# Row maxima of causal attention: a max pass over 11 and 9 slots in place of 7, turned by VectorE and sent in eight pieces by ScalarE's queue

## The reference

```python
def _L0_attn_ref(x, ids, Wq, Aq, Bq, Wk, Ak, Bk, Wv, Av, Bv, Wo, Ao, Bo):
    Q, K, V = multilora(x, ids, Wq, Aq, Bq), multilora(x, ids, Wk, Ak, Bk), multilora(x, ids, Wv, Av, Bv)
    Q, K, V = split(Q), split(K), split(V)              # (8, 16, 512, 32)
    Q, K = rope(Q), rope(K)
    scores = einsum('bhqd,bhkd->bhqk', Q, K) / sqrt(32)
    scores = where(causal, scores, -inf)
    attn = softmax(scores, axis=-1)
    out = einsum('bhqk,bhkd->bqhd', attn, V).reshape(b, s, 512)
    return multilora(out, ids, Wo, Ao, Bo)

def _L0_ffn_ref(hidden, ...):
    x = rmsnorm(hidden, ln1_w)
    mod = 0.1 * tanh(attention(x, Wq, Wk, Wv, Wo) @ A)  # the same causal attention, 16 heads of 32
    h = rmsnorm(hidden, ln2_w)
    gate = silu(h @ W_in.T + mod * (h @ A) @ B)
    return hidden + (gate * (h @ W_up.T)) @ W_down.T

x = layernorm(x + attn(x));  x = layernorm(x + ffn(x))
```

## Time and profile before

| | |
|---|---|
| median of 3 runs | 3022.44 us (3020.67 to 3022.64) |
| the profiled execution's own time | 3024.16 us |
| its span (first to last instruction) | 3022.3 us |
| TensorE (PE) busy | 2747.8 us, 91% |
| VectorE (DVE) busy | 1587.3 us, 53% |
| ScalarE (ACT) busy | 1337.3 us, 44% |
| GpSimd (POOL) busy | 644.2 us, 21% |
| mean granted TensorE clock | 0.947 of full speed |

### The profile page before, as it was taken

The page is one execution under the profiler, slowest core; times in us unless marked ns, Lnnn a source line. Parts: engine busy times, 40 slices in busy tenths (PEclk is TensorE's granted clock), DMA queues, the critical chain, the costliest instruction groups (busy, mean ns, idle before and its releaser), DMA issues. The chain is left out here.

```text
span 3022.3 us, 46154 instructions
## 1 busy us (share of the span) xinstructions
PE 2747.8 (91%) x13840; PEld 2183.9 (72%) x13840; DVE 1587.3 (53%) x4308; ACT 1337.3 (44%) x2755; POOL 644.2 (21%) x528
## 2 busy tenths in 40 slices
PE   5989998999848998999899996899999999999998
PEld 4778777877736776676677663688888888888886
DVE  3667666767644776767767764422222243333333
ACT  2667666766642556556555665411111131111111
POOL 5455555555421122112122112000000000000000
PEclk8999999999967999999999998899999999999999
DMA  5455545655544445454454542511111131111100
GB/s 137 98 119 136 111 117 126 138 112 121 129 121 108 97 109 121 91 117 109 96 125 100 106 100 45 180 45 43 47 61 48 46 103 43 44 57 43 44 28 28
DMA packets 173888, 276.05 MB, mean 91 GB/s; under 512 B 29204, under 2 KB 53524, under 8 KB 173076
## 3 DMA queue, kind: packets, MB, share of 16 engines
q1 hardware_dynamic: 170772, 260.58, 35.5%
q0 software_dynamic: 2304, 12.58, 1.2%
q10 hardware_dynamic: 640, 1.05, 0.1%
HBM read 97.04 MB, written 42.99 MB: 46 GB/s over the span
## 5 line engine op out<-in xcount | busy, mean ns | idle before, releaser
L2223 DVE TENSOR_TENSOR c_product<-c_up_ps,c_gate 128x512 f32<-128x512 f32 x128 | 88.6, 692 | 653.2 <-PE c_up_ps L2289 653.2
L2277 PE MATMUL c_gate_ps<-c_h_split,c_w_split 128*128 128x512 f32 x1536 | 380.7, 396 | 22.5 <-DVE c_w_split L2175 22.5
L2261 PE MATMUL c_down_ps<-c_w_split,c_product_split 128*128 128x512 f32 x1536 | 379.3, 396 | 0.0
L2289 PE MATMUL c_up_ps<-c_h_split,c_w_split 128*128 128x512 f32 x1536 | 378.1, 394 | 0.0
L2277 PEld LDWEIGHTS c_gate_ps<-c_h_split,c_w_split 128*128 128x128 f32 x1536 | 289.4, 188 | 94.8 <-issue 24.3
L2289 PEld LDWEIGHTS c_up_ps<-c_h_split,c_w_split 128*128 128x128 f32 x1536 | 287.9, 187 | 70.5
L2261 PEld LDWEIGHTS c_down_ps<-c_w_split,c_product_split 128*128 128x128 f32 x1536 | 288.5, 188 | 69.0
L281 ACT ACTIVATE b_prob_hi<-b_scores_t_ps 128x384 fp32r<-128x384 f32 (+1 forms) x384 | 200.2, 521 | 296.8 <-PE b_scores_t_ps L271 271.6
L289 DVE TENSOR_TENSOR a_prob_lo<-a_scores_t_ps,a_prob_hi 128x384 fp32r<-128x384 f32 (+1 forms) x384 | 226.1, 593 | 143.2 <-ACT a_scores_t_ps L282 134.6
L2147 ACT ACTIVATE c_gate<-c_gate_ps 128x512 f32<-128x512 f32 x128 | 76.4, 597 | 492.4 <-PE c_gate_ps L2284 492.4
L281 ACT ACTIVATE a_prob_hi<-a_scores_t_ps 128x384 fp32r<-128x384 f32 (+1 forms) x384 | 201.1, 524 | 203.1 <-PE a_scores_t_ps L271 188.1
(11 more groups left out here) (205 smaller groups left out, 4922.0 us busy)
## 6 DMA issues: line engine op xcount, KB each, us to landing
a_q_stack<-a_q_split SPq DMA_DIRECT2D x192, 128.0 KB, 3.2
a_k_stack<-a_k_split SPq DMA_DIRECT2D x192, 128.0 KB, 3.4
b_q_stack<-b_q_split SPq DMA_DIRECT2D x192, 128.0 KB, 3.3
b_k_stack<-b_k_split SPq DMA_DIRECT2D x192, 128.0 KB, 3.6
c_h_stage<-h_t SPq DMA_DIRECT2D x16, 1024.0 KB, 6.2
c_res<-x SPq DMA_DIRECT2D x16, 1024.0 KB, 5.6
c_w_stage<-in_mlp_w POOLq DMA_DIRECT2D x16, 768.0 KB, 4.6
stage<-in_x_t SPq DMA_DIRECT2D x8, 1024.0 KB, 6.4
```

Source lines behind the costliest of these rows:

```text
L2223: dve.tensor_tensor(product[:, bank, :], up_ps[:, bank, :], gate[:, bank, :], ALU.mult).then_inc(product_done, 1)
L2261: mm = pe.matmul(down_ps[:, t, :], product_split[:, kt % 2, a, t * P:t * P + P], w_split[:, w, kt, 2 * KC * P:], start=(kt == 0 and i == 0 ...
L2277: pe.matmul(gate_ps[:, bank, :], w_split[:, w, ft, c * 2 * P:c * 2 * P + P], h_split[run.pair][:, a, c, :], start=(c == 0 and w == 0 and a ...
L2289: mm = pe.matmul(up_ps[:, bank, :], w_split[:, w, ft, c * 2 * P + P:(c + 1) * 2 * P], h_split[run.pair][:, a, c, :], start=(c == 0 and w = ...
```

## The change

The row maxima are kept by head (`rowmax` is [128, 4 heads, 4 row tiles]). As soon as the 6 units of a *pair* of heads are done, `shift_made` (VectorE) negates and splits them (two instructions on 128x8) and transposes the [128, 32] tile in square blocks of 32, so that the 16 rows of a pair lie in each block of 32 partitions as 16 x 32 values. `shift_send` then issues 4 DMAs, one per block of partitions, each with 16 runs of 32 floats, on ScalarE's queue: for heads 0 and 1 in slot 8, for heads 2 and 3 in slot 1 of the next step. TensorE's transposes, ScalarE's copy and the one DMA go. `score_t_unit` waits for pair 0 at unit 0 and for pair 1 at unit 6. The max pass takes slots 1 to 11 in the first attention (one unit each, two in slot 11) and slots 1 to 9 in the second (1, 1, 2, 1, 1, 2, 1, 1, 2). In the second attention `low` moves: TensorE from slots 8 and 9 to slots 10 and 11 of step 4, ScalarE to slot 0 and VectorE to slot 1 of the step after; `mod` gets a buffer of its own, which takes away two waits.

```diff
+SHIFTS = P // 32 * 16
-def shift_split(dve, at, b, g):
+def shift_made(dve, at, b, g, pair):
     n = number(b, g)
-    dve.wait_ge(at.score_read, (n + 1) * UNITS)
-    at_least(dve, at.shift_turned, n)
-    dve.tensor_scalar(at.shift[:, :, 0:GH], at.rowmax[:, :, :], -1.0, None, ALU.mult).then_inc(at.shift_hi, 1)
...
+    m = n * 2 + pair
+    heads = slice(2 * pair, 2 * pair + 2)
+    apart(dve, at.ones_set, at.score_read, n * UNITS + (pair + 1) * (UNITS // 2))
+    at_least(dve, at.shift_turned, m)
+    dve.tensor_scalar(at.shift[:, pair, 0, :, :], at.rowmax[:, heads, :], -1.0, None, ALU.mult).then_inc(at.shift_hi, 1)
+    dve.wait_ge(at.shift_hi, m + 2)
+    dve.scalar_tensor_tensor(out=at.shift[:, pair, 1, :, :], in0=at.rowmax[:, heads, :], scalar=-1.0,
+                             in1=at.shift[:, pair, 0, :, :], op0=ALU.mult,
                              op1=ALU.subtract).then_inc(at.shift_ready, 1)
+    apart(dve, at.ones_set, at.shift_ready, m + 1)
+    at_least(dve, at.shifted[pair], n * SHIFTS)
+    dve.transpose(at.shift_t[pair][:, :],
+                  at.shift[:, :, :, :, :].rearrange("p a b c d -> p (a b c d)").bitcast(F32)).then_inc(
+        at.shift_turned, 1)
-def shift_turn(pe, at, eye, b, g):
...
-def shift_copy(act, at, b, g):
...
-def shift_send(act, at, b, g):
+def shift_send(sp, at, b, g, pair):
     n = number(b, g)
-    act.wait_ge(at.shift_copied, n + 1)
-    act.dma_start(at.q_stack[g % 2][SHIFT_ROW:STACK_ROWS, :, :].bitcast(F32),
-                  at.shift_row[0:2 * GH, :].bitcast(F32)).then_inc(at.shifted, 16)
+    sp.wait_ge(at.shift_turned, n * 2 + pair + 1)
+    target = at.q_stack[g % 2][SHIFT_ROW:STACK_ROWS, 2 * pair:2 * pair + 2, :].bitcast(F32).rearrange(
+        "r h (t c i) -> r h t c i", t=TT, c=P // 32)
+    for c in range(P // 32):
+        first = 32 * c + pair * 16
+        sp.dma_start(target[:, :, :, c, :],
+                     at.shift_t[pair][first:first + 16, :]).then_inc(at.shifted[pair], 16)
@@ score_t_unit
-    if k == 0:
-        pe.wait_ge(at.shifted, n * 16 + 16)
+    if k % (UNITS // 2) == 0:
+        pe.wait_ge(at.shifted[k // (UNITS // 2)], (n + 1) * SHIFTS)
@@ the two attentions
-SCORE_SLOTS = range(1, 8)
+        at = Attention(nc, ctx, "a", HD, 4, None, range(1, 12))
+        at = Attention(nc, ctx, "b", RANK, 3, (1, 1, 2, 3), range(1, 10))
@@ ScalarE, both attentions
-                    if slot == 9 and not (last and g == GROUPS - 1):
-                        shift_copy(act, at, *group(b, g, 1))
-                        shift_send(act, at, *group(b, g, 1))
+                    if slot == 8 and not (last and g == GROUPS - 1):
+                        shift_send(act, at, *group(b, g, 1), 0)
+                    if slot == 1 and not first:
+                        shift_send(act, at, b, g, 1)
@@ VectorE, both attentions
-                        for k in score_share(slot):
+                        for k in score_share(at, slot):
                             score_max(dve, at, rowmask, *group(b, g, 1), k)
-                        if slot == SCORE_SLOTS[-1]:
-                            shift_split(dve, at, *group(b, g, 1))
+                            if k % (UNITS // 2) == UNITS // 2 - 1:
+                                shift_made(dve, at, *group(b, g, 1), k // (UNITS // 2))
@@ TensorE, both attentions
-                    if slot == 9 and not (last and g == GROUPS - 1):
-                        shift_turn(pe, at, eye, *group(b, g, 1))
@@ second attention: ScalarE, VectorE, TensorE
                         if slot == 0:
+                            if has(b, 1):
+                                if not (isinstance(b, int) and b == 1):
+                                    act.wait_ge(z_out, (b - 1) * 32)
+                                low(b + 1)
                             value(b, 1)
-                    if g == 3 and slot == 11 and has(b, 2):
-                        low(b + 2)
+                    if g == 0 and slot == 1 and not zero and has(b, 1):
+                        low(b + 1)
-                    if g == 3 and slot in (8, 9) and has(b, 2):
-                        low(b + 2, share(3 * KC, 2, slot - 8))
+                    if g == 3 and slot in (10, 11) and has(b, 2):
+                        low(b + 2, share(3 * KC, 2, slot - 10))
```

89 lines of the change are left out of this document (34 added, 55 removed).

## The result

| | before | after |
|---|---|---|
| median | 3021.56 us (4 runs, 3018.33 to 3022.64) | 3146.69 us (4 runs, 3146.36 to 3147.25) |
| ratio | | 1.0416, 95% interval 1.0398 to 1.0434 |
| profiled span, granted clock | 3022.3 us, 0.947 | 3144.7 us, 0.931 |
| first attention, first to last exponent | 804 us | 900 us |
| second attention, the same | 888 us | 916 us |

The change makes the kernel 4.2% slower, 125 us; 3045 was forecast, and the range ended at 3075. Between the two profiled spans lie 122 us; the first attention grew by 96 and the second by 28, and the rest of the kernel is 1 to 2 us shorter. The direction was right and the size was not.

What follows compares the result with a forecast made beforehand. TensorE's list, busy nine tenths of both attentions, was taken as the bound. Terms -13 - 21 - 6 + 22 + 15 + 10 - 3 + 13 + 6 = +23 us gave 3045 us, range 3001 to 3075.

Steps and rivals of the forecast that it cites:

- What VectorE costs, the price of `shift_made`: Two small instructions and a transpose on VectorE: 0.65 us with waits, twice a step, for about 0.4 us before.
- Term 6: First attention, batch end: late units and shift_made before the jump, +10 us; second attention's pass end and `low`, -3 us.
- Term 7: Second attention, end of step 2: two units and longer shift_made work delay VectorE's norm factors, +13 us.
- term 4: First attention, steady steps, slots 8 and 1: ScalarE's four-issue bursts delay the exponents, +22 us.
- Term 5: Second attention, step 3: the burst in slot 1 passes straight through to TensorE, +15 us.
- Terms 1 and 2: TensorE gains: the four transposes go, -13 us, and the wait for the row maxima goes, -21 us.
- Term 3: First attention, step 2: the adapter's chain gets ahead as four max-pass units leave earlier slots, -6 us.
- Term 8: Second attention, step 1: VectorE finishes `low` in slot 1 after TensorE needs it, +6 us.
- D: Rival: ScalarE's issues wait while SyncE issues, about 1.2 us each, giving about 3125 us; chance 0.07.
- A: Rival: bursts hide because the wider pass starts VectorE's `lo_unit` earlier, giving about 3002 us; chance 0.17.
- C: Rival: ScalarE's issues cost only 0.34 us each, giving about 3016 us; chance 0.12.
- E: Rival: the last of four DMAs lands late and TensorE still waits at unit 0 or 6, about 3060 us; chance 0.04.

Runs made afterwards that it cites:

- e5: The changed kernel, wide pass kept, with shift_made's two small instructions written as one-input tensor_reduce with negation: 3089.5 us, ratio 1.0218.
- e1: The changed kernel with shift_made's first instruction as a two-input SCALAR_TENSOR_TENSOR in place of a TENSOR_SCALAR: 3140.6 us, ratio 1.0415.
- e9: e7 with shift_made in e5's one-input form: 2997.2 us, ratio 0.9920.
- e10: e5 (wide pass, one-input form) with the sends in pieces of two, in slots 7, 9, 0 and 3: 3065.5 us, ratio 1.0154.
- e3: The changed kernel with the max pass back in slots 1 to 7 in both attentions: 3054.7 us, ratio 1.0122.
- e7: e3 with the same eight DMAs a step sent in ones and twos (slots 7, 9, 10, 0 and 3): 3016.2 us, ratio 0.9973.
- e11: e9 with `low` of the second attention back in its old slots: 2989.0 us, ratio 0.9896.

## Why the prediction was wrong, step by step

**What VectorE costs, the price of `shift_made`: the step that failed.** I took "the small ones" at 0.18 us from one row, bounded them with 0.18 and 0.48 and came to 0.65 us for three instructions. Measured, from the start of the first to the end of the transpose in the first attention: 1.57 us in the median and up to 2.23, since the small ones wait up to 1.3 us for GpSimd. No term of the sum held this; e5 prices it at 60 us, of which 54 lie in the first attention, 36 as TensorE's longer busy time and 18 as its idle time. It was to be seen: the same line in the kernel before reads

```profile
L210 DVE TENSOR_SCALAR b_shift<-b_rowmax x32: 174/264/1278, 964.7 to 1844.8; 128x16 fp32r<-128x16 f32 x32
```

and a maximum of 1278 ns beside a minimum of 174, at one shape, is a resource that is not always free. I had read one row of a quiet place. That line is of the second attention; in the first, where most of the loss came, the same line stood at 174/175/458 and L212 at 174/176/1185, one long one in 32, so that the size could not be read there: the change moved `shift_made` to where GpSimd works. The Trainium skill, SBUF — State Buffer, section Who interferes with whom, says that a VectorE instruction with two SBUF inputs contends with a GpSimd instruction that reads SBUF, that in VectorE's 2-port modes, which a `tensor_scalar` can enter, whoever issues first keeps the shared port pair for the whole instruction and the other fully blocks, and that on trn2 `tensor_reduce` never contends. The trace agrees with the durations: e1's form 1.03 us in the median, L211's 1.05, e5's 0.16. Which mode L211 ran in no run shows.

**Terms 6 and 7, width.** +10 and +13 us, less 3 and 6. Measured, by e9 and e10: 28 us in the first attention and 34 in the second. Term 6 had the mechanism, units and a `shift_made` ahead of the jump; 1.6 us a jump was too little: VectorE is 2.0 us later there in e10 and 3.0 in the changed kernel, and slot 2 of the next batch 3.8 and 5.0. (And the standstill comes five times, not six.) Term 7 had the place (the end of step 2), but I stopped at one wait. The delay goes on: e10's step 3 takes 32.9 us against 29.0 of e9, with 10.2 us of waits on `b_q_split` at L1646 that neither e9 nor the kernel before has at this place, and step 2 31.6 against 29.5 (steps as the mean from exponent to exponent, batches 2 to 7). Term 7's own addition, 1.1 and 0.9 us, is 2.0 and not 1.9; this changes nothing. The gain that I had set against it, -3 us, did not show.

**Terms 4 and 5, the bursts.** +22 and +15 us, at 0.63 us an issue. The issues take

```profile
L231 ACTq DMA_DIRECT2D a_q_stack<-a_shift_t x256: 620/621/1241, 56.3 to 955.6; - x128
```

as assumed. From e5 to e10 the bursts are worth 0.64% (19 us) in the wide kernel, from e3 to e7 1.5% (45 us) with seven slots. The 37 lies between. In the wide kernel it is all term 4's: from e5 to e10 the first attention's window falls by 24 us (846 to 822), the second's does not fall (908 and 910); steps 3 and 4 of the first get 1.9 and 1.5 us shorter, where the term had 1.6. One burst in the changed kernel, ScalarE, step 3, slots 8 and 9:

```profile
489.92 0.49 ACT L274 ACTIVATE a_prob_hi<-a_scores_t_ps 128x384 fp32r<-128x384 f32 x1 [2.35 <-PE a_scores_t_ps L264]
490.00 0.62 ACTq L231 DMA_DIRECT2D a_q_stack<-a_shift_t  x1
490.30 0.49 ACT L275 ACTIVATE a_scores_t_ps<-a_scores_t_ps 128x384 f32<-128x384 f32 x1
490.65 2.00 ACTq L231 DMA_DIRECT2D a_q_stack<-a_shift_t  x3
...
493.26 0.59 ACT L274 ACTIVATE a_prob_hi<-a_scores_t_ps 128x512 fp32r<-128x512 f32 x1
```

Slot 9's exponent starts 3.34 us behind slot 8's; I had said 3.5 or more. Term 5 got its number right by luck: step 3 of the second attention grew by 2.0 us as forecast (30.9 to 32.9), but e10, without bursts, has the same 32.9. In the wide kernel the width alone does it, and the bursts add nothing to it; with seven slots they do, 31.4 us in e3 against 30.1 in e7. The waits on `prob_lo`, 78 us before and "some 130" in the prediction, came to 187, and the steady steps to 25.8 and 27.1 us from 21.8 and 22.1.

**Terms 1 and 2.** -13 and -21 us. The waits for the maxima are gone, 0.4 us of 20.9 are left. e11 keeps the transposes' gain and most of the other (6.6 us of waits for the maxima are back) and has little left of the four costs; it is 1.04% (31 us) faster than before, against the 34 of the two terms. This is the nearest that I have to a measurement of them. **Term 3**, -6 us: the wait on `low_stack` fell from 15.4 to 10.5. That the wide pass did this is not borne out: with the same pass it is about 14.5 us in e5 and e10. The number came near by luck.

**Term 8**, +6 us: 6.8 us in six waits ahead of step 1's slot 2, and e11 gained 0.24% (7 us by the ratios, 8 by the medians) over e9.

**The rivals.** D gave 3125 by another mechanism, issues that take turns; at a median of 0.621 us it did not happen, though the time came nearest. That a rival ends near the measured time is no evidence for it. Of the 512 issues 242 overlap one of SyncE's, and their median is 0.622 us, as against 0.621 of the others; but 19 of the 242 took 0.77 to 1.24 us, and none of the others over 0.73. The rule of the Trainium skill with which I had weighed D, in Perfetto Trace Analysis, section DMA Instruction — HWDGE (DVE, Sync), that an issue's profiled time holds the wait for a lock, may show in these 19; it does not make ScalarE's issues 1.2 us long, as D would have it. A needed 2.1 us of slack at slot 9; e7 shows that the issues can be hidden, but by moving them, not by a wider pass. C needed issues of 0.34 us, and E waits for the maxima, of which 0.4 us are left. No rival spoke of GpSimd.

Along the chain change, e5, e10, e9, e11, before, the ratios give GpSimd 60 us, bursts 19, width 71, `low` 7 and the gains -31. The sum is 126 us by construction (1.0416 is 126 us); by the intervals each part is good to 6 to 12 us, and what a part costs depends on which of the others are there: the bursts 19 us with the wide pass and 45 with seven slots. Against the prediction's +23, which missed by some 103 us, that is 60 too little for GpSimd, about 51 too little for width (it had 20), 1 for `low` and 9 for the gains (it had 40), less 18 too much for the bursts.

## What to carry to other kernels

Price a small VectorE instruction by the spread of its line, minimum to maximum, and by what GpSimd does at the place to which it moves. Here a TENSOR_SCALAR, or a form with two SBUF inputs, that began while GpSimd's TENSOR_TENSOR ran did not end before that did; `tensor_reduce` with negation did the same work in 0.16 and 0.17 us. Before spreading work over more slots to smooth an engine, ask what stands at the end of its list: with VectorE at some 70% busy, later units were late units, and a microsecond ahead of a jump was paid in full or more. Issues that came in fours stopped TensorE; the same issues in ones and twos, where ScalarE idled, cost nothing that could be told.

## What was not expected of the hardware

- A VectorE instruction of 8 elements a row took up to 1.30 us beside GpSimd's TENSOR_TENSOR of 512 (1.29 us), and a form with two inputs waits like one with a scalar; `tensor_reduce` and the block transpose (0.21 us, 210 to 215 ns in all 128) never did; 65 of e5's 128 first `tensor_reduce` ran wholly within a TENSOR_TENSOR of GpSimd.
- Behind an idle time of 2.27 us in TensorE's list, in the midst of a step that else ran at 1.00, its granted clock was 0.50 for over 2 us; with such waits the matmuls of the first attention took 38 us longer in all.
- VectorE's list stands still for 2.9 to 4.4 us at the program's jump, in the five kernels looked at, whether it comes there early or late.
